# A two-layer attention and MLP kernel in a software pipeline: other dates for the weights, other orders on every engine

## What is computed

```python
x = x + L0_xattn(layernorm(x), ctx, ctx)       # causal, 16 heads of 16, softmax over 128 keys
x = x + L0_ffn(layernorm(x), ...)              # x @ base_w.T + b, plus a LoRA of 8 experts, top 2 of a router
x = x + L1_xattn(layernorm(x), ctx, ctx)       # along the other axis: 8 heads, 256 queries and keys
x = x + L1_ffn(layernorm(x), w1, w2, gamma)    # RMS norm, 8-bit activations, ternary weights, gelu, 256-1024-256
```

## Time and profile before

| | us |
|---|---|
| median of 3 runs | 413.86 |
| lowest, highest | 408.65, 415.42 |
| the profiled execution, its own time | 415.81 |
| its span, first to last instruction | 413.4 |

### The profile page before, as it was taken

The page is one execution under the profiler, slowest core; times in us unless marked ns, Lnnn a source line. Parts: engine busy times, 40 slices in busy tenths (PEclk is TensorE's granted clock), DMA queues, the critical chain, the costliest instruction groups (busy, mean ns, idle before and its releaser), DMA issues.

```text
span 413.4 us, 9678 instructions
## 1 busy us (share of the span) xinstructions
PE 318.2 (77%) x3010; PEld 192.7 (47%) x3010; DVE 307.9 (74%) x838; ACT 264.4 (64%) x501; POOL 230.9 (56%) x449
## 2 busy tenths in 40 slices
PE   0047366497799899999999999999787578566883
PEld 0024244264465465665655665665443234234453
DVE  6432362759899687889997978897885574999983
ACT  2124153355577488789777876777465347988993
POOL 6257465838585557769656676235424113566534
PEclk9996796888899899999999999999996789999999
DMA  3675774976655738658757577623413400001111
GB/s 101 203 210 131 223 212 105 271 204 168 169 152 172 219 86 237 187 167 225 201 159 212 147 209 193 166 57 92 108 57 94 90 2 1 2 17 36 39 52 63
DMA packets 73137, 56.20 MB, mean 136 GB/s; under 512 B 5376, under 2 KB 62592, under 8 KB 73088
## 3 DMA queue, kind: packets, MB, share of 16 engines
q1 hardware_dynamic: 68896, 50.87, 44.8%
q10 hardware_dynamic: 4192, 4.73, 4.5%
HBM read 36.45 MB, written 18.87 MB: 134 GB/s over the span
## 4 chain that ended last, share of the span: by engine, by line
PE 45%; DMA 16%; DVE 12%; issue 9%; ACT 8%; SPq 6%; POOL 3%; ACTq 0%; POOLq 0%; DVEq 0%
DMA q<-max_t 8%; PE ps_u L1186 6%; PE ps_st L1155 6%; PE ps_s L1140 5%; DMA k<-k_parts 5%; PE ps_ff L1256 4%; PE ps_st L1122 3%; PE ps_st L1126 3%; PE ps_u L1169 3%; DVE max L1801 3%; PE ps_s L1104 2%; PE ps_t L1284 2%; PE ps_s L1108 2%; SPq L616 2%; DMA k_parts<-k_split 2%
## 5 line engine op out<-in xcount | busy, mean ns | idle before, releaser
L1801 DVE TENSOR_REDUCE max<-ps_s 128x2 f32<-128x512 f32 (+1 forms) x192 | 127.1, 685 | 49.0 <-PE ps_s L1108 28.0
L1507 ACT ACTIVATE p<-ps_st 128x512 f32<-128x512 f32 x128 | 71.9, 596 | 23.6 <-PE ps_st L1155 15.6
L1497 ACT ACTIVATE p<-ps_st 128x512 f32<-128x512 f32 x64 | 37.2, 597 | 30.3 <-PE ps_st L1126 29.9
L1140 PE MATMUL ps_s<-k,q 96*128 96x256 bf16 x256 | 51.2, 284 | 5.6 <-DMA k<-k_parts 3.2
L1155 PE MATMUL ps_st<-q,k 98*128 98x256 bf16 x256 | 48.0, 288 | 4.9 <-ACT p L1507 3.1
L1186 PE MATMUL ps_u<-p,v 128*32 128x256 f32 x512 | 39.5, 422 | 3.4 <-POOL v L874 3.4
L1122 PE MATMUL ps_st<-mask_k,ident_bf 128*128 128x512 bf16 x64 | 26.9, 421 | 18.3 <-DMA q<-max_t 17.5
L1155 PEld LDWEIGHTS ps_st<-q,k 98*128 98x128 bf16 x256 | 21.8, 102 | 20.9 <-issue 6.4
L1140 PEld LDWEIGHTS ps_s<-k,q 96*128 96x128 bf16 x256 | 20.3, 100 | 22.8 <-issue 10.9
L923 POOL TENSOR_SCALAR var<-mv 128x1 f32<-128x1 f32 x32 | 7.3, 229 | 41.8 <-DVE mv L1890 34.1
L1284 PE MATMUL ps_t<-ident_bf,q_split 128*128 128x128 bf16 x128 | 12.8, 259 | 21.6 <-POOL q_split L897 21.6
(11 more groups left out here) (147 smaller groups left out, 798.3 us busy)
## 6 DMA issues: line engine op xcount, KB each, us to landing
k_parts<-k_split SPq DMA_DIRECT2D x16, 512.0 KB, 4.1
q<-q_parts SPq DMA_DIRECT2D x32, 256.0 KB, 3.8
k<-k_parts SPq DMA_DIRECT2D x32, 256.0 KB, 3.6
kv_in<-in_kv SPq DMA_DIRECT2D x16, 256.0 KB, 3.7
q_parts<-q_t SPq DMA_DIRECT2D x16, 256.0 KB, 3.7
q<-q_parts SPq DMA_DIRECT2D x32, 128.0 KB, 3.9
k<-k_parts SPq DMA_DIRECT2D x32, 128.0 KB, 3.6
q_parts<-q_split SPq DMA_DIRECT2D x16, 256.0 KB, 2.8
```

The source lines that it names most:

```text
L1140: last = pe.matmul(out_[:, f * D:(f + 1) * D], q1[0:STK, odd, h * D + f * P:h * D + (f + 1) * P], k1[0:STK, odd, h * D:(h + 1) * D], start ...
L1497: act.activation(p0[:, g, :], ps_st[bank_of(ST_BANKS, f"s0t{g}")][:, :], ACT.Exp, scale=SCALE).then_inc(exp0_done[g], 1)
L1507: act.activation(p1[:, h, :], ps_st[bank_of(ST_BANKS, f"s1t{h}")][:, :], ACT.Exp, scale=SCALE).then_inc(exp1_done[h], 1)
L1801: dve.tensor_reduce(out_, src, AX.X, ALU.max, negate=True).then_inc(done, 1)
```

## The change

It has five parts.
1. The routed layer's weights are loaded in pieces at the ends of ScalarE's iterations 3, 4 and 5 with three semaphores, the late batches of `x` at 4 and 6 in place of 3 and 5, the MLP's weights at 5 and 7 in place of 4 and 6. The sums of the MLP's weights, the last statistics and the batch of the scales move one iteration later.
2. The lists of all five engines for the fill are new; those of the body and the drain are changed in part.
3. Stages of the MLP are moved by up to three iterations, and the drain has one iteration more.
4. `norm0` and `norm2` wait for the first of the three steps of the split of the batch before, not for all three.
5. Two pairs of semaphores are merged into one each.

The diff, cut: repeated waits and the parts of the lists that are not spoken of are left out. Lists are shown with the names alone.

```diff
-RMS = 17
-XN = 17
+RMS = 18
+XN = 16
-DEQUANT_IN = 20
+DEQUANT_IN = 23
-QUANT_IN = 20
+QUANT_IN = 21
-DEQUANT_HID = 27
+DEQUANT_HID = 30
-COPY_HID = 27
-DOWN = 28
-SCALE_OUTPUT = 30
-ADD_OUTPUT = 29
+COPY_HID = 28
+DOWN = 29
+SCALE_OUTPUT = 31
+ADD_OUTPUT = 31
-END = NB + 30
+END = NB + 31
-X_ITERATIONS = {0: 2, 1: 3, 3: 4, 5: 5}
-W_FF_ITERATION = 2
-W_LOADS = {4: 0, 6: 1}
-W_BATCH = 9 - FF
+X_ITERATIONS = {0: 2, 1: 3, 4: 4, 6: 5}
+FIRST_WEIGHTS, NEXT_WEIGHTS, GAMMAS = 3, 4, 5
+W_LOADS = {5: 0, 7: 1}
+W_BATCH = 10 - FF
...
 SP fill
-rows1 load_kv store_k load_v1 load_q0 rows0 load_k0 store_q1 load_k1 load_q1 store_q0
+load_kv store_k rows1 load_q0 load_k0 rows0 store_q1 load_k1 load_v1 load_q1 store_q0
 SP body
-load_kv rows1 store_k load_q0 rows0 load_v1 load_k0 store_q1 load_k1 load_q1 store_q0
+rows1 load_v1 load_kv store_k load_q0 rows0 load_k0 store_q1 load_k1 load_q1 store_q0
 SP drain
-load_kv store_q0 rows1 load_v1 store_k rows0 load_q0 store_q1 load_k0 load_q1 load_k1 store_out
+store_k rows1 rows0 load_q0 load_v1 store_q1 load_k0 load_k1 load_q1 load_kv store_q0 store_out
...
 TensorE fill
+scores1_t 6, turn_back, scores1 6, 2, 0, turn_u0, scores1 1, turn_gated, scores1_t 1, scores1 3,
+lora, pv1, turn_q0, scores1 7, scores0_t 1, 2, scores1 4, scores0 2, pv1, scores0 3, scores1_t 2,
+scores0_t 0, turn_max1, scores0_t 3, scores0 0, turn_xh1, scores0 1, turn_u1, pv0 1, pv1, ff,
+pv0 2, 3, 0, scores1 5, scores1_t 5, 0, 3, pv1, turn_max0, scores1_t 4, 7
 TensorE body, in part
-scores1_t 2, pv0 1, scores1 4, lora, scores0_t 0, scores0 2, pv0 2, scores0 3, turn_max1
+scores1_t 2, pv0 2, scores1 4, lora, scores0_t 0, scores0 2, scores0 3, pv0 1, turn_max1
 TensorE drain, in part
+down first; up after scores0_t 1; turn_in after scores0_t 2; turn_hid after scores1 3
 ScalarE fill, the start
-exp1 1, norm2_high, copy_max0, exp1 5, exp2, copy_max1, copy_u0, norm2, exp1 4, copy_gated, exp0 1, ...
+norm2_high, exp1 0, 7, norm2, exp2, copy_u0, copy_max0, copy_gated, copy_q0, norm0, exp1 5, exp0 1, ...
 VectorE fill
-weight_sum(0) after maxima1 4 at t == 6; stats0_group(5) last at t == 7
+weight_sum(0) last at t == 7
 VectorE body
-weight_sum(1) last at t == 8
+stats0_group(5) last at t == 8; weight_sum(1) last at t == 9
 GpSimd fill
-q1_mid q1_low place_v0 k_rest rstd1 k_mid k_low x1b rstd2 q0_rest q0_mid k_high q0_low q1_rest place_v1
+q1_mid q1_low k_rest place_v0 k_mid rstd1 k_low rstd2 q0_rest x1b place_v1 q0_mid k_high q1_rest q0_low
...
 def norm0(t):
     wait_rstd0(b)
-    act.wait_ge(q0_split_step, b * 3)
+    if later(b, 1):
+        act.wait_ge(q0_split_step, b * 3 - 2)
...
+def load_w_ff(f):
+    act.dma_start(wff_sb[:, f, :], w_ff[f * P:(f + 1) * P, :]).then_inc(w_ff_in, 16)
...
 ScalarE fill, the end
-if t == W_FF_ITERATION:
-    for dst, src in (base_b, w_ff, lora_b, router_b, attn_gamma, mlp_gamma):
-        act.dma_start(dst, src).then_inc(weights_in, 16)
+if t == FIRST_WEIGHTS:
+    act.dma_start(base_b_all[:, :], base_b.partition_broadcast(P)).then_inc(base_b_in, 16)
+    act.dma_start(router_b_all[:, :], router_b.partition_broadcast(P)).then_inc(w_ff_in, 16)
+    load_w_ff(0)
+if t == NEXT_WEIGHTS:
+    load_w_ff(1)
+    act.dma_start(lora_b_sb[:, :], lora_b).then_inc(lora_in, 16)
+if t == GAMMAS:
+    act.dma_start(attn_gamma_all[:, :], attn_gamma.partition_broadcast(P)).then_inc(lora_in, 16)
+    act.dma_start(mlp_gamma_all[:, :], mlp_gamma.partition_broadcast(P)).then_inc(lora_in, 16)
...
 def lora(t):
     pe.wait_ge(gated_copied, b + 1)
+    if isinstance(b, int) and b == 0:
+        pe.wait_ge(lora_in, 3 * 16)
```

More of the change, by code:

```diff
@@ L747, in fill, with body @@
             def fill(t, odd):
-                rows1(t, odd)
                 load_kv(t, odd)
                 store_k(t)
-                load_v1(t, odd)
+                rows1(t, odd)
+                load_q0(t, odd)
+                load_k0(t, odd)
+                rows0(t, odd)
+                store_q1(t)
+                load_k1(t, odd)
+                load_v1(t, odd)
+                load_q1(t, odd)
+                store_q0(t)
+            def body(t, odd):
+                rows1(t, odd)
+                load_v1(t, odd)
+                load_kv(t, odd)
+                store_k(t)
                 load_q0(t, odd)
@@ L1307, in fill @@
-                turn_gated(t)
-                scores0_t(t, odd, 1)
-                scores1(t, odd, 1)
-                pv1(t, 1, 0)
-                scores1_t(t, odd, 0)
-                scores0_t(t, odd, 2)
                 scores1(t, odd, 3)
+                lora(t)
+                pv1(t, 0, 0)
                 turn_q0(t)
                 scores1(t, odd, 7)
-                scores1_t(t, odd, 3)
-                turn_back(t)
+                scores0_t(t, odd, 1)
+                scores0_t(t, odd, 2)
@@ L1318, in fill @@
+                scores1(t, odd, 4)
+                scores0(t, odd, 2)
+                pv1(t, 1, 0)
+                scores0(t, odd, 3)
+                scores1_t(t, odd, 2)
+                scores0_t(t, odd, 0)
+                turn_max1(t)
+                scores0_t(t, odd, 3)
+                scores0(t, odd, 0)
+                turn_xh1(t)
+                scores0(t, odd, 1)
                 turn_u1(t)
                 pv0(t, odd, 1)
-                scores1(t, odd, 4)
-                lora(t)
@@ L1322, in fill @@
-                scores0_t(t, odd, 0)
-                scores0(t, odd, 2)
-                scores0(t, odd, 3)
-                turn_max1(t)
-                scores0_t(t, odd, 3)
-                turn_xh1(t)
-                scores0(t, odd, 0)
-                scores0(t, odd, 1)
+                pv1(t, 0, 1)
                 ff(t)
+                pv0(t, odd, 2)
                 pv0(t, odd, 3)
-                turn_max0(t)
-                pv1(t, 0, 0)
-                scores1_t(t, odd, 2)
-                scores1_t(t, odd, 5)
@@ L1336, in fill @@
-                scores1_t(t, odd, 7)
-                pv0(t, odd, 2)
                 pv0(t, odd, 0)
                 scores1(t, odd, 5)
-                scores1_t(t, odd, 6)
+                scores1_t(t, odd, 5)
+                scores1_t(t, odd, 0)
+                scores1_t(t, odd, 3)
+                pv1(t, 1, 1)
+                turn_max0(t)
+                scores1_t(t, odd, 4)
+                scores1_t(t, odd, 7)
             def body(t, odd):
@@ L1659, in fill @@
-                exp1(t, 0)
-                norm0(t)
-                norm0_high(t)
-                exp0(t, 3)
-                copy_u1(t)
-                exp1(t, 3)
-                exp0(t, 0)
-                exp1(t, 7)
+                norm2_high(t)
+                exp1(t, 0)
+                exp1(t, 7)
+                norm2(t)
+                exp2(t)
+                copy_u0(t)
+                copy_max0(t)
+                copy_gated(t)
+                copy_q0(t)
+                norm0(t)
@@ L2150, in body @@
                     clip_weight(1, (w1_q, w2_q)[1], (w1_sb, w2_sb)[1])
+                if isinstance(t, int) and t == 9:
+                    weight_sum(1)
+                if isinstance(t, int) and t == 8:
+                    stats0_group(5)
             def split_k0():
```

320 lines of the change are left out of this document (148 added, 172 removed).

## The result

| | before | after |
|---|---|---|
| median, us | 414.64 (4 runs) | 421.88 (4 runs) |
| lowest, highest | 408.65, 418.36 | 420.30, 423.28 |
| ratio after to before, 95% interval | | 1.0248, 1.0184 to 1.0312 |
| profiled execution, its span | 415.81, 413.4 | 420.94, 418.2 |

The account below looks back on a forecast made before the run. TensorE was taken to bound full iterations at 15.6 us, a chain of waits to pace the fill. Fill -10.5, VectorE's long extras +1.5, body 0 and drain +1.0 gave -8.0 us, so a median of 405.9, range 398 to 417.

Parts of the forecast that it names:

- loop through the query's store: Fill before: query transposed behind `scores0_t`, rows behind the query load, a closed loop of 15.6 us; the new order cuts it.
- The fill: Filling the pipeline: earlier start and shorter iterations give -10.5 us, bounds -15 and 0.
- VectorE's extras: `weight_sum(0)`, 2.25 us, moves into a busy stretch of VectorE at iteration 7: +1.5 us, range 0 to +2.2.
- the rows should land in about 3 us: Fill: key load issued about 1 to 2 us ahead of the maxima's rows, so they land nearer 2.70 than 6.85.
- Loop A: Fill: `scores0_t`, `scores0`, maxima, `turn_max0`, rows, then the next `scores0_t`; sum 12.4 us.
- Loop B: Fill, over two iterations: rows behind key load, that behind the key store's landing; 12.0, 14.1 or 16.0 us each.
- 7.6 us: Fill: time from the rows' landing to the maxima's transpose, 9.1 before, with query transposes and LoRA matmul moved ahead.
- The gammas: Fill, iteration 5: `lora` of batch 0 waits for their late load; 3.5 us longer, bounds 0 and 5.
- The full iterations: Body: orders change, nothing is added, TensorE stays at 15.6 us an iteration; 0, bounds +-2.
- The MLP part: Drain: `copy_hid` one stage later, `copy_hid` and `down` of batch 14 at the end; net +1.0 us, bounds 0 and +3.
- Rows behind the keys: Rival, fill: 384 KB of keys always ahead of the rows, 14.1 us an iteration, -3.9, time 410; chance 0.20.
- the one on the slower side: Rival, fill: `rows0` waits for the landing of that iteration's key store, about 17 us an iteration; +10, time 424; chance 0.09.

Follow-up runs that it names:

- mean of eight: Profiles of eight kernels with one and the same new fill: `turn_max0` of t = 8 at 120.0 to 126.0 us, 123.6 in the mean.
- Four buffers: The kernel after with four stack buffers in place of two for the first attention's query and key, first four batches: 413.52 us, ratio 1.0032.
- the lists alone: The kernel before with all five engines' lists of the full iterations from the kernel after, nothing else: 417.19 us, ratio 1.0108.
- one column: The kernel after with GpSimd's `add_output` adding one column in place of 256: 413.29 us, one run.

## Why the prediction was wrong

**Right.** The chain of the fill was read rightly, and the loop through the query's store went away; the first `scores0` came 4 us sooner and `turn_max0` of t = 2 at 26.1 in place of 29.9. The drain's first iterations stayed near 14 us: the last five from `turn_max1` to `turn_max1` took 14.2 us each, against 13.9.

**The fill (-10.5, with the +1.5 for VectorE's extras -9.0; measured -2.4 at t = 8 in the profiled execution and about -0.5 in the mean of eight).** The step that failed is "the rows should land in about 3 us". The loads that were to leave early were held by the buffer of batch b - 2, which Loop A and Loop B leave out, and so left in front of the rows: 5.03, 7.15, 4.20 and 5.07 us in place of 2.7 to 3. Four buffers show it for two of the four landings; the other two took 7.27 and 7.52, and why is open. Three more terms were wrong. From the rows' landing to `turn_max0` I had 7.6 us; by the chain it is 8.7 (48.28 to 57.0), 8.2 (66.43 to 74.6) and 9.8 (81.11 to 90.9). Four matmuls of scores take 0.22 us where the granted clock is full and 0.43 where it is half, as the chain of the kernel with four buffers has them at 46 and at 63 us, and the windows of after have the clock at 0.77 and 0.71; I left it as it was. In the kernel before, the query's transposes and the LoRA product ran at half clock behind the rows' landing, from 67.2 to 69.7, and all groups of scores behind them at 0.22. In the kernel after, scores stand there, at 0.43 until 70.07. So taking 0.85 and 0.6 off the 9.1 us saved about nothing of it, and the LoRA product is 1.09 us in the chain of before, not 0.6. And the gain of the first rows was given back at t = 3, 42.1 as before (39.9 to 42.1 in the eight traces), behind a key store of 6.37 us that met the biases and the first half of `wff`. The first rows stand behind the key load that waits for this store, and I had 1 us for that. With the rows ahead of it `turn_max0` of t = 3 came at 37.6 to 38.8 in four traces. The gammas, 3.5 in the sum, cost one wait of 1.0 us, since the rows came late in any case.

**The full iterations (0, bounds +-2, measured +1.6 in the profile and, for the lists alone, about +3.5 in time).** "TensorE has no idle time to give or lose" was wrong in its second half: an engine that is never idle can always lose. By the times it did; where is not shown. In the profile TensorE's new order asks for rows that haven't landed, 6.4 us of waits from t = 8 to 16 in place of 1.1. I looked at the bank that `pv0` 2 waits for, and not at how long after `turn_max0` and `turn_max1` the list comes to the scores that need their rows.

**The MLP part (+1.0, bounds 0 and +3, measured +4.5).** I summed instructions outside of VectorE's full stretch and took their durations as constant. VectorE was full, 22.9 of 23.5 us, and the new order made the same 152 instructions 3.8 us longer (59.9 to 63.7). 2.3 of these are shown to come from VectorE's products beside GpSimd's addition (61.4 with one column). TensorE's clock, 0.98 before and 0.91 after, was not in the sum at all, and its share was not measured.

**Rivals.** Rows behind the keys (410) named a part of what happened, the queue ahead of the rows, with the wrong cause: the rule on ring order of the Trainium skill, "DMA: Bandwidth & Descriptors", section "Queues, rings and completion order", agrees with slow landings behind loads, but with the keys behind them the rows still took 7.06 and 5.13 us. No rival had the loss: the one on the slower side was placed in the fill, and the loss came from the two stages that I had costed at 0 and +1.0.

## What to carry over

When you cut a wait, ask of each transfer behind it what else it waits for; a double buffer freed by the very stage that waits for the transfer closes the loop again, and shows in the waits of the issuing engine. In a stretch where one engine is full, a new order costs what it makes the instructions longer, not only what it moves. A stage without idle time can only be hurt by new orders, so 0 is one end of its range and not its middle.

## What was not expected of the hardware

- VectorE and GpSimd make each other's instructions longer: a product of 128x256 takes 0.28 us alone and 0.72 beside GpSimd's addition, a maximum of 128x1 on GpSimd 0.21 and 0.58, the addition itself 0.72 and 1.23. A reduction on VectorE beside the same addition takes 1.22 us, no more than alone.
- Rows of 4 KB took 1.7 to 7.95 us to land in these traces, as the queue and the other engine's queue were empty or not.
